# Sandwich network of four blocks on one core: order of work in the block attention and in the three-layer gated network

## The chip, the cores and the metric

One core of one Trainium2 chip. The metric is the device time of one execution of the whole program in microseconds; before the change the median of three runs is 6237.31 us (6226.17 to 6241.25). All data is float32.

## What is computed

The input `x` has 8 batches of 512 rows with 128 features. Four blocks follow one another, each an attention and then a feed-forward part, and each part `f` is applied as `x = x + layernorm(f(layernorm(x)))`. Only the first block is touched by the change. Its two parts, cut to what matters:

```python
def _L0_attn_ref(x, ...):                       # 16 heads of 8 features
    q = rmsnorm(proj(wq_w, wq_b), qn_w)
    k = rmsnorm(proj(wk_w, wk_b), kn_w)
    v = proj(wv_w, wv_b)
    allowed = (i[None, :] <= i[:, None]) & (i[:, None] - i[None, :] < WINDOW)   # WINDOW = 32
    scores = jnp.einsum('bhqd,bhkd->bhqk', q, k) * scale
    attn = jax.nn.softmax(jnp.where(allowed[None, None], scores, -jnp.inf), axis=-1)
    out = jnp.einsum('bhqk,bhkd->bhqd', attn, v)
    return out.transpose(0, 2, 1, 3).reshape(b, l, d) @ wo_w.T + wo_b

def _L0_ffn_ref(x, ...):                        # D_IN = 128, D_HID = 512
    h = jax.nn.silu(_tlin(x, w1_w, w1_s)) * _tlin(x, w2_w, w2_s)
    h = jax.nn.gelu(_tlin(h, h1_w, h1_s), approximate=False)
    h = jax.nn.gelu(_tlin(h, h2_w, h2_s), approximate=False)
    return _tlin(h, w3_w, w3_s)
```

## The kernel before

The whole `x` stays in SBUF. Stages run one after the other, each in a block of its own, and inside a stage each engine has its own list of instructions, written out by hand; an engine waits on semaphores that other engines raise. No planner chooses an order. A stage runs over 8 batches (`B`), a batch being four tiles (`TB`) of 128 rows.

**Block attention** (`stage_attn0`, unrolled over 8 batches and their 32 tiles). The window of 32 keys lets a block of 32 queries see only 64 keys. For a batch, VectorE normalizes `x` (`input_stats`, `input_norm`, with the inverse root on GpSimd), PE transposes it (`turn_input`, L968) into PSUM bank 2, ScalarE copies it (`copy_input`, L1090), PE makes queries and keys (`project`, L975) in banks 2 and 3, VectorE adds the bias and clips (`unscaled`, L1176 and L1180), ScalarE squares (`squares`), VectorE sums (`mean_squares`, L1185 to L1187), ScalarE takes roots (`roots`, L1098), VectorE divides (`scaled`, L1191 and L1192), PE transposes queries and keys back (`turn`, L986), and ScalarE copies the queries once and the keys eight times, each time with other heads masked to zero (`queries` L1102, `keys` L1107). The values are made by `project_v` (L994), again in banks 2 and 3, and copied by ScalarE (`values`, L1114). For a tile, PE makes the scores (`scores`, L1006) in banks 0 and 1, VectorE adds the mask and takes the maximum (`masked`, L1199 and L1202), GpSimd subtracts it (`shifted`, L946), ScalarE takes the exponential (`probs`, L1120), PE transposes (`transposes`, L1015), ScalarE copies (`probs_turned`, L1124), PE multiplies with the values (`values`, L1028) and VectorE divides by the sums (`weighted`, L1207 and L1208). At the end of a batch come `turn_output` (L1040), `copy_output` (L1129), `output` (L1046, bank 2), `result` (L1213) and the output norm (`post`). Two things are waited for across batches: the first scores of a batch wait for all its key copies (`kz_ready`), and `turn` waits until `result` has read bank 2 (`y_read`).

```python
            for n in range(N):
                b, t = n // TB, n % TB
                if t == 2 and b + 1 < B:
                    turn(b + 1)
                if n + 1 < N:
                    scores(n + 1)
                if t == 0:
                    project_v(b)
                if n:
                    values(n - 1)
```

**Gated layer network** (`stage_ffn0`, a loop over the 8 batches on each engine). PE: eight up products in pairs (`w1` and `w2`, L354; chunk `m` of the pair goes to banks `2m % 4` and the next), 16 products of the first hidden layer (L363), the transposes of the next batch's input (L254), 16 of the second, and 16 small down products into bank 4 (L376). ScalarE applies silu to one of a pair (L401), VectorE multiplies it by the other (L443) and so frees that bank; ScalarE applies gelu to the hidden layers (L409). VectorE then takes the result (L451), normalizes it and adds it to `x` before it comes to the next batch's first pair. Silu and gelu need different function tables in ScalarE. `pe.drain()` before a semaphore makes PE wait until its products have left it.

## Time and profile before

| | us |
|---|---|
| median of three runs | 6237.31 |
| lowest and highest run | 6226.17, 6241.25 |
| the profiled execution, its own time | 6221.95 |
| its span | 6220.1 |
| block attention in it, first product to last addition to `x` | 17.04 to 380.27 |
| gated layer network in it, first transpose to last addition | 397.46 to 761.41 |
| PE, VectorE, ScalarE, GpSimd busy in the span | 5232.3, 3558.8, 2288.6, 2504.0 |

The span runs from the first instruction to the last on the slowest core (there is one). A row of a timeline gives the start, the length, the engine, the line of the kernel, what is written from what, how many instructions it merges, and in brackets how long the engine had been idle and who ended that. PE's matmuls in float32 are recorded as two each. DVE is VectorE, ACT ScalarE, POOL GpSimd; PEclk is the clock granted to TensorE, 1.00 being full.

### The profile page before, as it was taken

What the parts mean: (1) busy time and instruction counts of PE and PEld (TensorE: products, weight loads), DVE (VectorE), ACT (ScalarE), POOL (GpSimd) and SP (SyncE); (2) the same over time, 40 slices, a digit from 0 to 9 for tenths busy, and PEclk for the clock granted to TensorE, in tenths of its full rate; (3) what the DMA queues carried; (4) which work ended last, traced back from release to release, by engine and by line L of the source; (5) the groups of instructions that cost most, each with busy time, mean ns of one, the idle gap of its engine ahead of it and who ended that gap; (6) DMA issues with size and microseconds to landing.
All of it is one profiled execution on the core that took longest, in us unless ns stands there. A gap on an engine that the chain in (4) does not pass through costs nothing. (4 is left out here: it accounts for less than half of the span.)

```text
span 6220.1 us, 182529 instructions
## 1 busy us (share of the span) xinstructions
PE 5232.3 (84%) x72132; PEld 3776.6 (61%) x72132; DVE 3558.8 (57%) x9531; ACT 2288.6 (37%) x4072; POOL 2504.0 (40%) x2788
## 2 busy tenths in 40 slices
PE   4568868888848888898888888898679999787998
PEld 2334345555536777777777777777346666576776
DVE  4631268787865565555565565565545545685333
ACT  3532236666623333333333333333222333111333
POOL 1210014444436666666666666666300000573000
PEclk8789989999969999999999999999789999898999
DMA  0000010000000000000000000000010000000000
GB/s 19 2 20 0 2 42 1 0 0 0 0 7 11 11 11 12 12 13 12 11 12 11 11 12 11 11 12 11 7 42 0 0 0 0 4 1 28 0 0 13
DMA packets 29562, 58.05 MB, mean 9 GB/s; under 512 B 7312, under 2 KB 14240, under 8 KB 28704
## 3 DMA queue, kind: packets, MB, share of 16 engines
q1 hardware_dynamic: 28960, 48.86, 2.6%
q8 instruction: 520, 8.52, 0.6%
q14 instruction: 82, 0.67, 0.0%
HBM read 46.75 MB, written 2.10 MB: 8 GB/s over the span
## 5 line engine op out<-in xcount | busy, mean ns | idle before, releaser
L617 PEld LDWEIGHTS psum<-m_wd,m_h 128*128 128x128 f32 x6144 | 805.6, 192 | 485.4 <-issue 484.3
L617 PE MATMUL psum<-m_wd,m_h 128*128 128x128 f32 x6144 | 819.6, 277 | 95.3 <-remote 69.6
L2183 POOL TENSOR_TENSOR e_kd<-e_kd,e_tail 128x512 f32<-128x512 f32 x325 | 368.7, 1135 | 567.7 <-PE psum L2290 554.2
L607 PE MATMUL psum<-xT,m_wa 128*128 (+1 forms) x1032 | 544.3, 610 | 8.4 <-remote 8.4
L607 PE MATMUL psum<-xT,m_wb 128*128 (+1 forms) x1032 | 532.8, 598 | 0.0
L784 DVE SCALAR_TENSOR_TENSOR m_acc<-psum,m_combine,m_acc 128x128 f32<-128x128 f32 x1440 | 403.3, 342 | 224.0 <-PE psum L617 211.0
L544 POOL TENSOR_TENSOR m_h<-m_td,m_tb 128x512 f32<-128x512 f32 x258 | 328.6, 1274 | 468.6 <-DVE m_tb L812 468.6
L2320 PE MATMUL psum<-e_T,e_N 64*64 64x32 f32 x10400 | 407.1, 232 | 67.7 <-remote 66.3
L2320 PEld LDWEIGHTS psum<-e_T,e_N 64*64 64x64 f32 x10400 | 370.6, 148 | 113.2 <-issue 110.0
L2290 PE MATMUL psum<-e_kd,e_k 64*64 64x64 f32 x10400 | 420.1, 237 | 0.3
L143 POOL TENSOR_SCALAR m_post_rstd<-m_post_mv 128x4 f32<-128x4 f32 x27 | 6.2, 228 | 990.7 <-DVE m_post_mv L133 990.7
L2290 PEld LDWEIGHTS psum<-e_kd,e_k 64*64 64x64 f32 x10400 | 372.4, 149 | 6.9 <-issue 1.2
L805 DVE SCALAR_TENSOR_TENSOR m_h<-psum,m_bb,m_ta 128x512 f32<-128x512 f32 x258 | 193.2, 749 | 308.4 <-ACT m_ta L705 305.2
L607 PEld LDWEIGHTS psum<-xT,m_wb 128*128 128x128 f32 x1032 | 199.3, 193 | 253.5 <-issue 253.5
L705 ACT ACTIVATE m_ta<-psum,m_ba 128x512 f32<-128x512 f32 x258 | 177.2, 687 | 458.9 <-PE psum L607 458.8
L2341 PE MATMUL psum<-e_Z,e_TT 64*64 64x32 f32 x8320 | 296.7, 221 | 25.0 <-DVE e_Z L2693 21.1
L2585 ACT ACTIVATE e_T<-psum 128x256 f32<-128x256 f32 x325 | 125.6, 386 | 514.4 <-PE psum L2341 514.4
L2693 DVE COPY e_Z<-psum 64x256 f32<-64x256 f32 x325 | 135.9, 418 | 301.8 <-PE psum L2320 301.5
L2341 PEld LDWEIGHTS psum<-e_Z,e_TT 64*64 64x64 f32 x8320 | 267.5, 135 | 48.7 <-issue 33.5
L699 ACT ACTIVATE m_h<-psum,m_ba 128x512 f32<-128x512 f32 x258 | 177.3, 687 | 288.3 <-PE psum L600 288.3
L2177 POOL TENSOR_TENSOR e_k<-e_k,e_tail 128x256 f32<-128x256 f32 x390 | 281.2, 721 | 0.0
L600 PE MATMUL psum<-m_normed,m_wa 128*128 128x512 f32 x516 | 268.9, 604 | 6.2 <-remote 6.2
(434 smaller groups left out, 11884.4 us busy)
## 6 DMA issues: line engine op xcount, KB each, us to landing
e_w<-in_e_w SPq DMA_DIRECT2D x66, 321.0 KB, 2.9
m_wa<-in_m_wa SPq DMA_DIRECT2D x12, 512.0 KB, 7.5
m_wd<-in_m_wd SPq DMA_DIRECT2D x12, 512.0 KB, 8.7
m_wb<-in_m_wb SPq DMA_DIRECT2D x8, 512.0 KB, 8.8
f_h<-in_f_h SPq DMA_DIRECT2D x2, 1024.0 KB
out<-x SPq DMA_DIRECT2D x1, 2048.0 KB, 8.7
f_w<-in_f_w SPq DMA_DIRECT2D x3, 256.0 KB
g_w<-in_g_w SPq DMA_DIRECT2D x3, 256.0 KB
```

The costliest lines, as they stand in the source:

```text
L544: g.tensor_tensor(h[:, j, :], td[:, j, :], tb[:, j, :], ALU.mult).then_inc(h_ready[j], 1)
L600: pe.matmul(c.ps[u % 4][:], wa[q][:, j, :], nrm[:, e % 2, :], start=True, stop=True).then_inc(a_ready[u % 4], 1)
L607: pe.matmul(c.ps[i][:], w[q][:, j, :], xb, start=True, stop=True).then_inc(a_ready[i], 1)
L617: r = pe.matmul(c.ps[4 + e % 2][:, t * P:(t + 1) * P], h[:, u % DEPTH, t * P:(t + 1) * P], wd[u // UQ][:, u % UQ, :], start=(m == 0 and t ...
L699: a.activation(h[:, j, :], c.ps[u % 4][:], ACT.Relu, bias=ba[:, u:u + 1]).then_inc(h_ready[j], 1)
L784: r = v.scalar_tensor_tensor(to[:, t, :], c.ps[4 + e % 2][:, t * P:(t + 1) * P], comb[:, t, e:e + 1], acc[:, t, :], ALU.mult, ALU.add)
L805: v.scalar_tensor_tensor(h[:, j, :], c.ps[2 * k + 1][:], bb[:, u:u + 1], ta[:, j, :], ALU.add, ALU.mult).then_inc(h_ready[j], 1)
L2177: return g.tensor_tensor(even(k[:], m), even(src[:], m), gate, ALU.mult)
L2183: return g.tensor_tensor(both_odd(dst[:], m), both_odd(src[:], m), gate.unsqueeze(1).broadcast_to((P, 2, nb, m)), ALU.mult)
L2290: r = pe.matmul(c.psum[half(h), G_, chunk(u)], keys[half(h), chunk(u)], both_odd(gated[half(h), :, chunk(u)], 1 << l), start=True, stop=True)
L2320: r = pe.matmul(c.psum[half(1 - h), Z_, u * HC:(u + 1) * HC], N[half(h), l - 1, chunk(u)], even(T[half(h), chunk(u)], 1 << l), start=True, ...
L2341: r = pe.matmul(even(c.psum[half(h), T_, chunk(u)], 1 << l), left[half(h), chunk(u)], Z[half(h), u, :], start=False, stop=False, skip_grou ...
```

## The change

In block attention every engine's list is rewritten. Scores stand two tiles ahead of the transposes instead of one, on PE, VectorE (`masked`) and GpSimd (`shifted`). `turn` of the next batch moves from the third tile to the end of the first; the key copies are spread over the second tile; `project_v` of the next batch moves up into the third tile, before it is needed; `project` moves to the fourth tile, and belongs to the batch after next. The input transposes go to bank 3 in place of bank 2. Output projection, result and output norm come a batch later. In the gated layer network the first pair of up products of the next batch stands in front of the down products, and VectorE and ScalarE do that pair's work at the end of the turn; the scaling of the result, its norm and the addition move into the next batch's turn, behind three of its four pairs. Two semaphores are added there for the banks of the second product of a pair. No operation on data is dropped; one pair of up products, with one silu and one multiplication, is added for a ninth batch that nobody reads.

```diff
             pre.pe(pe, 0)
+            pe.wait_ge(pre.xT_ready, 1)
+            pe.sem_clear(pre.xT_ready)
+            up(0, c.xT[:, 0:L])
             with pe.Fori(0, B) as b:
...
+                for m in range(1, HC):
+                    up(m, c.xT[:, bass.ds(b * L, L)])
                 for n, w in enumerate((h1, h2)):
...
+                pe.wait_ge(pre.xT_ready, 1)
+                pe.sem_clear(pre.xT_ready)
+                up(0, c.xT[:, bass.ds((b + 1) * L, L)])
                 pe.wait_ge(h_ready[2], HC)
...
+            with v.Fori(1, B) as b:
+                ch.reset()
+                for m in range(1, HC):
+                    gated(m)
+                pre.dve_first(v, ch, b + 1)
+                scaled()
                 post.dve_stats(v, ch, lambda t: y[:, t, :])
-                post.dve_add(v, ch, b, lambda t: y[:, t, :])
+                pre.dve_last(v, ch, b + 1)
+                post.dve_add(v, ch, b - 1, lambda t: y[:, t, :])
+                first_gated()
...
             def turn(b):
                 pe.wait_ge(qk_ready, b + 1)
-                if b >= 2:
-                    pe.wait_ge(y_read, b - 1)
+                pe.wait_ge(xT_ready, min(b + 2, B))
+                if b >= 3:
+                    pe.wait_ge(y_read, b - 2)
...
             def project_v(b):
-                pe.wait_ge(xT_ready, min(b + 2, B))
+                pe.wait_ge(kz_ready, b + 1)
...
             for n in range(N):
                 b, t = n // TB, n % TB
+                if t == 3 and b + 2 < B:
+                    project(b + 2)
+                if n + 2 < N:
+                    scores(n + 2)
+                if t == 0 and b >= 2:
+                    output(b - 2)
                 if t == 2 and b + 1 < B:
-                    turn(b + 1)
-                if n + 1 < N:
-                    scores(n + 1)
-                if t == 0:
-                    project_v(b)
+                    project_v(b + 1)
                 if n:
                     values(n - 1)
+                if t == 0 and b + 2 < B:
+                    turn_input(b + 2)
+                transposes(n)
                 if t == 0 and b + 1 < B:
-                    pe.wait_ge(vz_ready, b + 1)
-                    project(b + 1)
-                transposes(n)
...
+                    turn(b + 1)
+                if t == 3 and b:
+                    turn_output(b - 1)
...
             copy_input(0)
+            copy_input(1)
             squares(0)
...
                 if t == 1 and b + 1 < B:
-                    roots(b + 1)
-                if t == 2 and b + 1 < B:
                     queries(b + 1)
-                    keys(b + 1, range(HP // 2))
-                probs_turned(n)
+                    keys(b + 1, range(2))
                 if n + 1 < N:
                     probs(n + 1)
...
+                if t == 1 and b + 1 < B:
+                    keys(b + 1, range(2, 6))
...
+                probs_turned(n)
+                if t == 1 and b + 1 < B:
+                    keys(b + 1, range(6, HP))
```

Three places of the order, word for word. **Block attention on PE, from `turn` (a_qk) to `project` (a_wqk).** Names are what is written and read: a_qk queries and keys, a_kz masked keys, a_wv the value weights, a_xn the normalized input, a_o the attention output. Before:

```order
L986 MATMUL psum<-ident,a_qk 128x128 x8
L1006 MATMUL psum<-a_kz,a_qT 32x512 x8
L1028 MATMUL psum<-a_vz,a_probsT 32x18 x32
L1015 MATMUL psum<-ident,a_probs 128x128 x8
L1006 MATMUL psum<-a_kz,a_qT 32x512 x8
L1028 MATMUL psum<-a_vz,a_probsT 32x18 x32
L1015 MATMUL psum<-ident,a_probs 128x128 x8
L968 MATMUL psum<-ident,a_xn 128x128 x4
L1006 MATMUL psum<-a_kz,a_qT 32x512 x8
L994 MATMUL psum<-a_wv,a_xTp 64x64 x32
L1028 MATMUL psum<-a_vz,a_probsT 32x18 x32
L975 MATMUL psum<-a_wqk,a_xTp 128x256 x4
```

In the changed kernel:

```order
L1036 MATMUL psum<-ident,a_qk 128x128 x8
L1056 MATMUL psum<-a_kz,a_qT 32x512 x8
L1078 MATMUL psum<-a_vz,a_probsT 32x18 x32
L1065 MATMUL psum<-ident,a_probs 128x128 x8
L1056 MATMUL psum<-a_kz,a_qT 32x512 x8
L1044 MATMUL psum<-a_wv,a_xTp 64x64 x32
L1078 MATMUL psum<-a_vz,a_probsT 32x18 x32
L1065 MATMUL psum<-ident,a_probs 128x128 x8
L1024 MATMUL psum<-a_wqk,a_xTp 128x256 x4
```

From `turn` to the next batch's first scores there is now one turn of values and transposes with one scores product before it, as before; but behind those first scores the value products (a_wv) follow at once, where a tile, the input transposes (a_xn) and the second tile's scores stood between. The output transposes and the output projection, which stood ahead of `turn`, stand elsewhere.

**Block attention on ScalarE and VectorE, around the exponentials' table load and around `scaled` (a_qk).** ScalarE before, then changed:

```order
L1120 ACT_TABLE_LOAD
L1120 ACTIVATE a_probs<-a_probs 128x1024
L1102 ACTIVATE a_qT<-psum,a_nw 128x512
L1107 ACTIVATE a_kz<-psum,a_headmask 128x512 x4
L1124 ACTIVATE a_probsT<-psum 128x1024
L1120 ACTIVATE a_probs<-a_probs 128x1024
L1107 ACTIVATE a_kz<-psum,a_headmask 128x512 x4
```

```order
L1153 ACTIVATE a_qT<-psum,a_nw 128x512
L1158 ACTIVATE a_kz<-psum,a_headmask 128x512 x2
L1171 ACT_TABLE_LOAD
L1171 ACTIVATE a_probs<-a_probs 128x1024
L1158 ACTIVATE a_kz<-psum,a_headmask 128x512 x4
L1175 ACTIVATE a_probsT<-psum 128x1024
L1158 ACTIVATE a_kz<-psum,a_headmask 128x512 x2
```

The table load and the exponential now stand among the key copies. VectorE before, then changed:

```order
L1199 TENSOR_TENSOR a_probs<-psum,a_window 128x1024
L1202 TENSOR_REDUCE a_max<-a_probs 128x16
L1207 RECIPROCAL a_rec<-psum 128x16
L1208 TENSOR_TENSOR a_o<-psum,a_rec 128x128
L1191 RECIPROCAL a_rstd<-a_rstd 128x128
L1192 TENSOR_TENSOR a_qk<-a_raw,a_rstd 128x1024
L1213 TENSOR_TENSOR a_y<-psum,a_bo 128x512
```

```order
L1254 TENSOR_TENSOR a_probs<-psum,a_window 128x1024
L1257 TENSOR_REDUCE a_max<-a_probs 128x16
L1246 RECIPROCAL a_rstd<-a_rstd 128x128
L1247 TENSOR_TENSOR a_qk<-a_raw,a_rstd 128x1024
L1262 RECIPROCAL a_rec<-psum 128x16
L1263 TENSOR_TENSOR a_o<-psum,a_rec 128x128
L1268 TENSOR_TENSOR a_y<-psum,a_bo 128x512
```

`weighted` (a_rec, a_o) stood between the maximum and `scaled`, and now stands behind it, with `result` (a_y) last in both.

**Gated layer network on PE, the end of a turn of the loop** (f_w the up and down weights, ISA a drain or a wait with a clear). Before, from the drain behind the second hidden layer:

```order
L366 ISA
L371 ISA
L373 ISA
L376 MATMUL psum<-f_w,f_hid 128x128 x16
L345 REGISTER_ALU
L345 COMPARE_AND_BRANCH
```

Changed:

```order
L379 ISA
L384 ISA
L358 ISA
L359 ISA
L359 MATMUL psum<-xT,f_w 128x512
L358 ISA
L359 MATMUL psum<-xT,f_w 128x512
L387 ISA
L389 ISA
L392 MATMUL psum<-f_w,f_hid 128x128 x16
L366 REGISTER_ALU
L366 COMPARE_AND_BRANCH
```

The pair of up products stands between that drain and the down products.

## Rows read from the trace of the kernel before

**Rows 1.** The stage windows of one batch, attention and gated layer (window, length, busy by engine, PEclk, DMA, GB/s).

```profile
197.00:238.00 41.00, 23.17 (x449) 15.16 (x448) 24.44 (x50) 20.59 (x26) 10.11 (x8) 0.79 0.01 2
534.20:578.60 44.40, 39.65 (x116) 18.93 (x116) 9.12 (x30) 11.41 (x15) 2.53 (x4) 1.00 0.00 0
```

**Rows 2.** PE's timeline over one batch of block attention (start, length, what, xcount, idle before).

```profile
207.19 1.94 PE L986 MATMUL psum<-ident,a_qk 128*128 128x128 f32 x8 [6.50 <-DVEq L1215]
...
219.15 1.96 PE L1006 MATMUL psum<-a_kz,a_qT 64*32 64x512 f32 x16 [5.85 <-ACT a_kz L1107]
...
226.69 1.11 PE L968 MATMUL psum<-ident,a_xn 128*128 128x128 f32 x4 [3.23 <-DVE a_xn L155]
...
229.62 2.08 PE L994 MATMUL psum<-a_wv,a_xTp 128*64 128x64 f32 x64
...
234.02 1.99 PE L975 MATMUL psum<-a_wqk,a_xTp 128*128 128x256 f32 x8 [1.64 <-ACT a_vz L1114]
```

**Rows 3.** PE's timeline at the two ends of block attention.

```profile
68.95 3.61 PE L975 MATMUL psum<-a_wqk,a_xTp 128*128 128x256 f32 x8 [3.36 <-ACT a_vz L1114]
...
95.88 1.96 PE L1006 MATMUL psum<-a_kz,a_qT 64*32 64x512 f32 x16 [5.66 <-ACT a_kz L1107]
...
311.65 3.56 PE L994 MATMUL psum<-a_wv,a_xTp 128*64 128x64 f32 x64
...
343.67 1.96 PE L1006 MATMUL psum<-a_kz,a_qT 64*32 64x512 f32 x16 [6.43 <-ACT a_kz L1107]
...
355.80 1.09 PE L1006 MATMUL psum<-a_kz,a_qT 64*32 64x512 f32 x16
...
359.66 1.09 PE L1006 MATMUL psum<-a_kz,a_qT 64*32 64x512 f32 x16
```

**Rows 4.** ScalarE's timeline in the same batch.

```profile
196.82 1.05 ACT L1120 ACTIVATE a_probs<-a_probs 128x1024 f32<-128x1024 f32 x1
...
199.32 1.28 ACT L1098 ACT_TABLE_LOAD   x1
...
200.84 1.00 ACT L1124 ACTIVATE a_probsT<-psum 128x1024 f32<-128x1024 f32 x1
...
209.17 2.42 ACT L1107 ACTIVATE a_kz<-psum,a_headmask 128x512 f32<-128x512 f32 x4 [0.17 <-PE psum L986]
```

**Rows 5.** VectorE's timeline, the first batch and the same later one.

```profile
50.95 1.22 DVE L1192 TENSOR_TENSOR a_qk<-a_raw,a_rstd 128x1024 f32<-128x1024 f32 x1
...
195.02 1.22 DVE L1176 TENSOR_TENSOR a_raw<-psum,a_bqk 128x1024 f32<-128x1024 f32 x1 [3.04 <-PE psum L975]
196.40 0.69 DVE L1180 TENSOR_SCALAR a_raw<-a_raw 128x1024 f32<-128x1024 f32 x1
198.85 1.22 DVE L1185 TENSOR_REDUCE a_rstd<-a_sq 128x128 f32<-128x1024 f32 x1 [1.75 <-ACT a_sq L1094]
...
200.50 1.22 DVE L1199 TENSOR_TENSOR a_probs<-psum,a_window 128x1024 f32<-128x1024 f32 x1
...
203.00 0.25 DVE L1207 RECIPROCAL a_rec<-psum 128x16 f32<-128x16 f32 x1
...
203.72 0.95 DVE L1191 RECIPROCAL a_rstd<-a_rstd 128x128 f32<-128x128 f32 x1
204.71 1.44 DVE L1192 TENSOR_TENSOR a_qk<-a_raw,a_rstd 128x1024 f32<-128x1024 f32 x1
```

**Rows 6.** GpSimd's timeline, same batch.

```profile
203.17 1.90 POOL L946 TENSOR_TENSOR a_probs<-a_probs,a_max 128x1024 f32<-128x1024 f32 x1 [9.82 <-DVE a_max L1202]
```

**Rows 7.** PE's timeline in one batch of the gated layer.

```profile
540.90 2.84 PE L354 MATMUL psum<-xT,f_w 128*128 x6 [2.10 <-DVEq L445]
...
557.86 0.65 PE L254 MATMUL psum<-ident,f_pre_y 128*128 128x128 f32 x4 [0.38 <-remote]
...
573.84 3.83 PE L376 MATMUL psum<-f_w,f_hid 128*128 128x128 f32 x32 [1.08 <-remote]
578.66 3.69 PE L354 MATMUL psum<-xT,f_w 128*128 x8 [0.98 <-remote]
```

More of the change, by code:

```diff
@@ L317, in stage_ffn0 @@
     free = [s(f"bank{i}_free") for i in range(4)]
+    gate_ready = [s(f"gate{i}_ready") for i in range(2)]
     t_ready = [s(f"silu{i}_ready") for i in range(2)]
@@ L332, in _ @@
             pre.pool(g, ch, 0)
-            with g.Fori(0, B) as b:
+            pre.pool(g, ch, 1)
+            with g.Fori(1, B) as b:
                 ch.reset()
@@ L382, in _ @@
                 pe.sem_clear(free[i])
+            pe.wait_ge(h_ready[0], 1)
+            pe.sem_clear(h_ready[0])
             pe.wait_ge(y_free, 1)
             pe.sem_clear(y_free)
-            pre.drain_pe(pe)
+            pe.wait_ge(pre.t_free, 1)
+            pe.sem_clear(pre.t_free)
         @block.scalar
@@ L413, in _ @@
                         pre.act(a, b + 1)
+                silu(0)
             pre.drain_act(a)
@@ L431, in _, with gated, first_gated, scaled @@
                 v.sem_inc(t_free[i], 1)
-            pre.dve(v, ch, 0)
-            with v.Fori(0, B) as b:
-                ch.reset()
+            def gated(m):
+                i = (2 * m + 1) % 4
+                v.wait_ge(gate_ready[i // 2], 1)
+                v.sem_clear(gate_ready[i // 2])
+                v.wait_ge(t_ready[m % 2], 1)
+                v.sem_clear(t_ready[m % 2])
+                v.scalar_tensor_tensor(hid[0][:, m, :], c.ps[i][:], s2[:, m:m + 1], t_s[:, m % 2, :],
+                                       ALU.mult, ALU.mult).then_inc(h_ready[0], 1)
+                d = v.drain()
+                d.then_inc(free[i], 1)
+                v.sem_inc(t_free[m % 2], 1)
+            def first_gated():
                 v.wait_ge(h_free[0], 1)
                 v.sem_clear(h_free[0])
-                for m in range(HC):
-                    i = (2 * m + 1) % 4
-                    v.wait_ge(ready[i], 1)
-                    v.sem_clear(ready[i])
-                    v.wait_ge(t_ready[m % 2], 1)
-                    v.sem_clear(t_ready[m % 2])
-                    v.scalar_tensor_tensor(hid[0][:, m, :], c.ps[i][:], s2[:, m:m + 1], t_s[:, m % 2, :],
-                                           ALU.mult, ALU.mult).then_inc(h_ready[0], 1)
-                    d = v.drain()
-                    d.then_inc(free[i], 1)
-                    v.sem_inc(t_free[m % 2], 1)
-                pre.dve(v, ch, b + 1)
+                gated(0)
+            def scaled():
                 v.wait_ge(y_ready, 1)
@@ L1153, in _ @@
                 if t == 0 and b + 1 < B:
-                    squares(b + 1)
+                    roots(b + 1)
+                if t == 0 and b + 2 < B:
+                    copy_input(b + 2)
+                if t == 1 and b + 1 < B:
+                    keys(b + 1, range(2, 6))
                 if t == 2 and b + 1 < B:
-                    keys(b + 1, range(HP // 2, HP))
+                    values(b + 1)
                 if t == 3 and b + 2 < B:
-                    copy_input(b + 2)
+                    squares(b + 2)
+                probs_turned(n)
+                if t == 1 and b + 1 < B:
+                    keys(b + 1, range(6, HP))
+                if t == 3 and b:
+                    copy_output(b - 1)
             copy_output(B - 1)
@@ L1237, in _ @@
             masked(0)
+            masked(1)
+            unscaled(1)
+            input_stats(2)
+            input_norm(2)
             for n in range(N):
```

137 lines of the change are left out of this document (77 added, 60 removed).

## Prediction

> **What bounds the kernel now.** I read the stage windows first, then the PE timeline of the two touched stages, then the timelines of the engines that PE waits for. The windows show two different stages [rows 1]. In block attention a batch takes 41.0 us and no engine is full: PE 23.2, VectorE 24.4, ScalarE 20.6, GpSimd 10.1 us, with the granted clock at 0.79. So a chain over several engines bounds it. In the gated layer network PE is busy 39.65 of 44.4 us at clock 1.00: PE bounds it, and only its gaps can be won.
>
> The attention chain is seen by following each long PE gap to its releaser [rows 2]. `turn` starts at 207.19 after 6.50 idle, released by VectorE's `result` (L1215). The next batch's first scores start at 219.15, after 5.85 idle for the last key copy of ScalarE. Then one tile's work and a wait for the normalized input (3.23) follow before the value products at 229.62; `project` follows at 234.02, when ScalarE has copied the values. 41.03 us before the next `turn` is the last one, so I can cut the cycle into legs: turn to first scores 11.96; first scores to value products 10.47; value products to VectorE's bias addition 6.43 (195.02 in the earlier batch [rows 5], so 236.05 here); and from that addition to `turn` 12.17 (195.02 to 207.19). They add up to 41.03.
>
> **Part 1: block attention, per batch.** I lay out the same cycle in the changed order.
>
> *Turn to first scores.* From the start of `turn` to the first key copy stays 1.98 (207.19 to 209.17). ScalarE's queue then holds two key copies (1.21, half of the 2.42 for four), the exp table load (1.28), an exponential (1.05, about 1.0 net, since its successor starts early), four key copies (2.42), a `probs_turned` (1.00), two key copies (1.21) [rows 4]. The exponential's input comes from a tile that GpSimd finished before; the transposes behind `probs_turned` are on PE by then. Sum 1.98 + 8.12 + 0.06 hand-off = 10.16. What goes is the wait between the two halves of the keys; what is new is the table load on this path, which stood beside a GpSimd wait. The load before the roots takes 1.28 and the next but one instruction stands 1.52 behind its start, so nothing follows it [rows 4]. *The Trainium skill, "ScalarE: Activation LUTs", section "What ACT_TABLE_LOAD costs", adds a drain of about 1.38 us to each 1.28 us load; by that, an estimate, each batch would cost 1.4 more and the forecast would be some 8 us later. This trace has no room for it.*
>
> *First scores to VectorE's bias addition.* The scores take 1.96. The value products follow at once: 2.08 usually, 3.56 in the one batch where they ran at the lower of the two clock levels (1.2 GHz instead of 2.4) [rows 2, 3]. The 1.96 of the scores is that level too (1.09 at the other), and in the changed order the value products stand 2.0 us behind the long gap, where they stood 2.9 us behind one (226.69 to 229.62). I take 3.2, nearer the slow row, and keep both ends. From their end to `project` 2.32 (229.62 + 2.08 to 234.02); values and transposes of a tile fit in there. `project` 1.99 plus hand-off 0.04. Sum 1.96 + 3.2 + 2.32 + 2.03 = 9.51. Gone is everything that stood between the first scores and the value products.
>
> *Bias addition to the next turn, all on VectorE* [rows 5]. Addition 1.38 (195.02 to 196.40); clip 0.83 (0.69 and the usual 0.14 to the next); mask, maximum and `weighted` of a tile 3.22 (200.50 to 203.72); sums 1.65 (198.85 to 200.50), their squares being ready while the tile is worked on; a second mask, maximum and weighted 3.22; reciprocal, `scaled` and `result` up to the release of PE 3.47 (203.72 to 207.19). Sum 13.77. That is 1.6 more than the 12.17 of before: two tiles are served now, where one was, but a wait for squares is gone. On top comes contention that the rows show: `scaled` took 1.22 with GpSimd idle (50.95) and 1.44 at 204.71, when GpSimd's subtraction (203.17 to 205.07) still ran; it ended 1.08 behind that. In the changed order `weighted` (0.72) no longer stands between the maximum and `scaled`, so `scaled` starts 0.72 earlier against the same subtraction. If it again ends 1.08 behind, it takes 2.16: +0.72 [rows 5, 6]. At the low end this is 0. Leg: 14.49.
>
> Period: 10.16 + 9.51 + 14.49 = **34.2 us**. The roots' result is due 0.2 us before VectorE wants it, so that wait is hidden, barely; each engine's own work (24.4 at most) stays below. Low end: value products 2.08 and no contention, 32.4. High end: 3.56, and `project` at 3.61 as in the first batch [rows 3]: 36.1.
>
> From batch 1's first scores (95.88) to batch 7's (343.67) there are six periods, 247.8 us [rows 3]. Six at 34.2 are 205.2: **-42.6**. At the start the second batch's input transposes and their copy stand ahead of `turn` and of the squares: +1. At the end the last batch's first scores stand one tile earlier in the list, so one more tile follows them, 3.86 at the tail's pace (355.80 to 359.66), and two output norms are left instead of one, mostly beside it: +4 (0 to 8). The first batches have no `result` and norm yet, which I price at nothing to -2.5. Attention: **-37.6**.
>
> **Part 2: gated layer network** [rows 7]. The first pair of up products moves in front of the down products. (a) The wait of 2.10 in the middle of the up products goes: VectorE came to the first pair only after norm and addition of the last batch. Now it does the pair under the down products (3.83), ScalarE's silu table load included, and result and norm run under the 14 us of hidden products (543.7 to 557.86). Seven times: -14.7. (b) The 1.08 before the down products, a wait for the last gelu, is covered by the pair (2 x 0.87), but the drain ahead of the pair costs what the same drain costs ahead of the transposes, 0.38: saved 0.7 in seven batches, -4.9. (c) In the last batch the pair for nobody takes 1.74 + 0.38 in place of 1.08: +1.0. (d) The 0.98 between down products and up products, drain and loop branch, stays. What is late next: VectorE must finish the next input's norm before the transposes, some 19 us after the turn begins; its work of a whole batch is 9.1 [rows 1]. The silu and gelu loads are as many as before. **-18.6**, with -12 if (b) and part of (a) come back.
>
> Sum: -37.6 - 18.6 = **-56.2**. Against the profiled execution (6221.95) that is 6165.8. That execution lies 15.4 under the median and even under the fastest of the three runs, so I apply the difference to the median: 6237.3 - 56.2 = **6181**.
>
> **The rivals.**
>
> *The clock takes more of it.* Long gaps remain before the first scores and before `turn`, and after each the rows show 1.2 GHz. If most of the chain's PE work stays there, the period is the 36.1 above: six times 1.9 more, 11.4, so 6192. For it: the granted clock of 0.79 and the slow row of 3.56. Against: 2.08 and 1.99 are the usual rows behind gaps of the same size. *The Trainium skill, "TensorE: Matmul & The Clock Gate", part 4, says that transposes do not count as activity for the clock, which speaks for this rival in a stage so rich in them.*
>
> *One half doesn't work.* In the gated network the 2.10 could turn into another wait, since the pair's bank must be freed by ScalarE and VectorE out of the same turn; then only attention gains: 6181 + 18.6 = 6200. Nothing in the rows asks for it: both engines idle there.
>
> *Slower.* One mechanism: engines work in order, and the lead of two tiles puts `masked(n+2)` ahead of `weighted(n-1)` on VectorE, and scores ahead of values on PE. Should each of them wait on the other's newest tile, the lead overlaps nothing, and each tile is a full round: scores 1.96, mask and maximum 2.50, GpSimd 1.90, exponential 1.05, transposes and values at most 2.32 together, copy 1.00, `weighted` 0.72, in all 11.4, four times 45.8, and the key copies (4.84) and the table load (1.28) come in series as ScalarE holds them before the exponential: 51.9 a batch. Six times 10.6 over the 41.3 that the six now take each, +64, +5 at the ends, -18.6: 6287. It decides from a period of some 43.5, where the six periods eat up the gated network's gain. Against it: walked through, only one long wait per batch (for the keys) blocks the scores.
>
> **How the numbers follow.** Forecast, period near 34 and the gated network's gain: 0.72. Clock rival 0.19. Half of it missing 0.06. Slower 0.03. The first three lie over 18.7 us (0.3%, about what a measurement of this kernel can tell from no change) below the median, the third by twice that; with a doubt left for a smaller gain: faster 0.94, same 0.03, slower 0.03. Range: low end, period 32.4 (-10.8), first batches -2.5, tail nothing, and a few us between medians: 6158. High end: the clock rival and half of the gated gain missing, 6202.
>
> **What would show it.** In the changed profile: first scores of the steady batches about 34 us apart; `turn` still released by `result`, and the first scores by the last key copy some 10 us after `turn`; value products directly behind the scores, at 3 us or more if the clock holds low; `scaled` near 2.16; in the gated network a turn of 41.6 us, no wait for VectorE between up products, 0.4 before the moved pair, down products at once behind it. The forecast is wrong if the scores are released by something other than the keys, if the period exceeds 36.1 or falls under 32.4, or if a wait over 1 us stands between hidden products.

## The result, and the profile after

The changed kernel takes 6155.83 us (median of four runs, 6151.69 to 6163.73) against 6231.74 (four runs, one more than were on record ahead of it, 6220.64 to 6241.25): ratio 0.988, 95% interval 0.9859 to 0.9902. The profiled execution took 6151.69 us, its span 6149.9. It is faster, as predicted, and by more than the range allowed: 6155.8 lies 2.2 us below the range's low end of 6158 and 25 us below the forecast of 6181.

A stage is counted below from its first weight transfer to the next stage's first, in SyncE's timeline, the last one to the transfer of the output.

| us | block attention | gated layers | the eight other stages |
|---|---|---|---|
| before | 369.67 | 380.98 | 5449.0 |
| after | 326.62 | 359.03 | 5443.5 |
| difference | -43.1 | -22.0 | -5.5 |

The windows of the changed kernel: attention stage, one batch of it, gated stage, one turn of it, and the delta stage (gated delta attention of a later block, whose code the change does not touch). Columns as in [rows 1]; the busy times are those of PE's products, PE's weight loads, VectorE, ScalarE and GpSimd.

```profile
11.63:338.25 326.62, 178.65 (x3586) 121.32 (x3586) 209.92 (x402) 164.53 (x201) 81.07 (x64) 0.85 0.01 3
220.06:253.91 33.85, 21.39 (x449) 14.85 (x449) 24.23 (x49) 20.31 (x25) 10.14 (x8) 0.85 0.01 2
338.25:697.28 359.03, 319.14 (x936) 154.94 (x936) 74.48 (x253) 93.88 (x123) 22.32 (x34) 0.97 0.02 8
443.44:484.75 41.31, 39.34 (x117) 19.11 (x117) 8.89 (x30) 11.41 (x15) 2.65 (x4) 1.00 0.00 0
1783.68:4308.59 2524.91, 2242.47 (x55182) 1819.03 (x55182) 1487.67 (x3407) 912.49 (x2020) 1603.49 (x1909) 0.94 0.04 12
```

An attention batch takes 33.85 us instead of 41.03, with the same VectorE and ScalarE work (24.2 and 20.3 us busy, 24.4 and 20.6 before). PE is busy 21.4 us in it, 23.2 before, at the higher granted clock; the rest of what went is waiting. PE's timeline over that batch, to be held against [rows 2], and the first scores of the second and the last batch [rows 3]:

```profile
96.00 1.96 PE L1056 MATMUL psum<-a_kz,a_qT 64*32 64x512 f32 x16 [4.16 <-ACT a_kz L1158]
...
220.06 1.94 PE L1036 MATMUL psum<-ident,a_qk 128*128 128x128 f32 x8 [6.66 <-DVEq L1270]
...
230.10 1.38 PE L1056 MATMUL psum<-a_kz,a_qT 64*32 64x512 f32 x16 [4.48 <-ACT a_kz L1158]
231.41 3.33 PE L1044 MATMUL psum<-a_wv,a_xTp 128*64 128x64 f32 x64
...
237.15 1.96 PE L1024 MATMUL psum<-a_wqk,a_xTp 128*128 128x256 f32 x8 [0.72 <-ACT a_vz L1165]
...
298.08 1.96 PE L1056 MATMUL psum<-a_kz,a_qT 64*32 64x512 f32 x16 [4.37 <-ACT a_kz L1158]
```

`turn` to first scores is 10.04 us. The value products now follow the scores at once; the 3.23 us wait of before is gone. From 96.00 to 298.08 there are six periods in 202.08 us, where there were 247.8. In the later profiles of the same two kernels they are 202.1 to 203.7 us in four of the change and 245.6 to 245.8 in three of before, which have no batch like the one of 42.5 us at the end of [rows 3]. The last leg is VectorE's; from its timeline, and GpSimd's, in the same batch:

```profile
239.30 1.22 DVE L1231 TENSOR_TENSOR a_raw<-psum,a_bqk 128x1024 f32<-128x1024 f32 x1
...
249.97 2.16 DVE L1247 TENSOR_TENSOR a_qk<-a_raw,a_rstd 128x1024 f32<-128x1024 f32 x1
...
253.01 0.69 DVE L1268 TENSOR_TENSOR a_y<-psum,a_bo 128x512 f32<-128x512 f32 x1
```

```profile
249.16 1.90 POOL L989 TENSOR_TENSOR a_probs<-a_probs,a_max 128x1024 f32<-128x1024 f32 x1 [3.07 <-DVE a_max L1257]
```

ScalarE's timeline shows the table load that came onto the path between turn and scores:

```profile
223.31 1.28 ACT L1171 ACT_TABLE_LOAD   x1
224.60 1.06 ACT L1171 ACTIVATE a_probs<-a_probs 128x1024 f32<-128x1024 f32 x1
225.57 2.41 ACT L1158 ACTIVATE a_kz<-psum,a_headmask 128x512 f32<-128x512 f32 x4
```

PE's timeline in one gated turn, against [rows 7]:

```profile
443.44 5.41 PE L359 MATMUL psum<-xT,f_w 128*128 x12 [0.88 <-remote]
448.69 13.90 PE L376 MATMUL psum<-f_hid,f_h 128*128 128x512 f32 x32
...
478.37 1.98 PE L359 MATMUL psum<-xT,f_w 128*128 x4 [0.49 <-remote]
480.19 3.73 PE L392 MATMUL psum<-f_w,f_hid 128*128 128x128 f32 x32
484.75 5.41 PE L359 MATMUL psum<-xT,f_w 128*128 x12 [0.83 <-remote]
```

Six products of three pairs run through without the 2.10 us wait, and the down products stand directly behind the moved pair. Down product to down product is 41.35 to 41.39 us in all seven turns; before it was 46.15 once and 44.41 to 44.46 six times.

So both halves did what was forecast, within some microseconds. The open questions were where the surplus of 25 us comes from, whether the lead of two tiles or only the new placement does the work, and which leg limits next.

### The profile page after: what moved, and what is told of

The parts are those of the page before. It is cut to its first block and busy times, and to the rows that moved or that the text cites. A ratio compares the mean times of both kernels' runs of the same rounds, so it can differ in the third digit from the quotient of the medians.

```text
span 6149.9 us, 182566 instructions
## 1 busy us (share of the span) xinstructions
PE 5217.9 (85%) x72136; PEld 3775.9 (61%) x72136; DVE 3560.4 (58%) x9532; ACT 2290.1 (37%) x4074; POOL 2504.0 (41%) x2788
## 5 line engine op out<-in xcount | busy, mean ns | idle before, releaser
L2382 PE MATMUL psum<-e_T,e_N 64*64 64x32 f32 x10400 | 407.7, 232 | 63.9 <-remote 63.2
L2382 PEld LDWEIGHTS psum<-e_T,e_N 64*64 64x64 f32 x10400 | 371.6, 149 | 108.9 <-issue 105.1
L2403 PE MATMUL psum<-e_Z,e_TT 64*64 64x32 f32 x8320 | 298.4, 221 | 30.7 <-DVE e_Z L2755 23.8
```

The lines of the kernel that those rows point to most:

```text
L2382: r = pe.matmul(c.psum[half(1 - h), Z_, u * HC:(u + 1) * HC], N[half(h), l - 1, chunk(u)], even(T[half(h), chunk(u)], 1 << l), start=True, ...
L2403: r = pe.matmul(even(c.psum[half(h), T_, chunk(u)], 1 << l), left[half(h), chunk(u)], Z[half(h), u, :], start=False, stop=False, skip_grou ...
```

## The experiments

**The halves alone, and both kernels again.** `same_again` is the kernel before; `full_again` the changed one; `attn_only` takes every list of the new attention and the old gated network; `gated_only` the reverse. The edit in each half is that part of the diff shown above.

> The kernel before with a blank line added, so the same instructions. Theory A (what the change won beyond its two stages is scatter between executions): ratio 1.000 within 0.2%, and the profile's untouched stages differ from those of the first profile of before by as much as the 5 us that were gained there in the changed kernel, the longest stage (2529 us) by up to 4 us. Theory B (the untouched stages really run faster behind the changed ones): the untouched stages repeat here within 1 us in all.

> Only the attention half of the change. Theory: the attention stage takes 326.6 us (369.7 before, so -43), the gated stage about 381 as before, the total -43 +- 5, ratio 0.993. Its steady batches 33.9 apart. Theory B would find the untouched stages 5 us shorter here too. Rival on the clock: the first two turns of the gated stage (46.2 and 46.1 us before, 44.4 later) become short by what the attention stage leaves behind, then the gated stage takes 377.

> Only the gated half. Theory: the gated stage takes 359 us (381.0 before, so -22), a turn 41.4, the attention stage 369.7 as before, total -22 +- 5, ratio 0.9965. If the slow first two turns are a matter of what the attention stage leaves behind, they stay slow here and the gated stage gains 18 to 19 only; if of the 2.10 wait between up products, they are gone here.

> The whole change again (a blank line added). Theory: attention 326.6, gated 359.0, untouched stages within 5 us of either profile; ratio 0.989 +- 0.002, that is -65 to -75; if the profile's two stages are all that is won, the ratio over many runs comes nearer to -65 (0.9896) than to the -76 first measured (0.988).

Ratios are to the kernel before, run beside them (median 6243.58 us).

| | median us (range) | ratio, 95% | attention | gated | eight others |
|---|---|---|---|---|---|
| same_again | 6245.29 (6232.73 to 6256.71) | 1.0002, 0.9992 to 1.0012 | 368.12 | 381.40 | 5480.4 |
| attn_only | 6184.24 (6182.36 to 6190.8) | 0.9903, 0.9889 to 0.9918 | 328.20 | 381.41 | 5458.8 |
| gated_only | 6208.61 (6200.69 to 6222.62) | 0.9944, 0.9931 to 0.9958 | 370.39 | 359.25 | 5465.1 |
| full_again | 6164.59 (6148.56 to 6173.63) | 0.9872, 0.9856 to 0.9888 | 329.13 | 358.45 | 5454.5 |

The two stages are independent: each half gains in its own stage what the whole gains there. But the medians win more than the stages: 79.0 us against 61.9 (the two stages of `same_again` less those of `full_again`). Each half does the same for itself: `attn_only` wins 59.3 us, 39.9 of them in the attention stage, and `gated_only` 35.0, 22.2 of them in the gated stage. So some 13 to 19 us lie outside the touched stage with either half, and 17 with both: they don't add up like the stages. Neither theory of `same_again` foresaw that kernel's own untouched stages to differ by 31 us between two profiles (5449.0 and 5480.4). The difference lies in stages with the same code; it is taken up at the end of this section.

**Is it the lead of two tiles?** `lead_one` keeps every new placement and gives back the lead, on PE, VectorE and GpSimd.

```diff
-                if n + 2 < N:
-                    scores(n + 2)
+                if n + 1 < N:
+                    scores(n + 1)
```

> The changed kernel with scores, masked and shifted one tile ahead instead of two; every other move stays. Theory: the lead matters, since on ScalarE the key copies and the roots stand behind an exponential whose subtraction is then made in the same turn: turn to last key 13.9 in place of 10.0; value products at once behind it; addition to turn 18.2 in place of 14.7 (the roots come 4.6 behind the mask), period about 39.6, the stage about 38 us longer. Rival (the gain comes from placing turn and the value products alone): period 34 or less.

Its one run took 6251.82 us, with the new gated network in it; the seven of the kernel before beside it took 6225.8 to 6247.09, median 6236.04. The attention stage is what tells: 405.34 us, some 37 more than before's, with a period of 44.1. From PE's, ScalarE's and VectorE's timelines:

```profile
220.78 1.94 PE L1035 MATMUL psum<-ident,a_qk 128*128 128x128 f32 x8 [5.83 <-DVEq L1268]
...
234.80 3.68 PE L1043 MATMUL psum<-a_wv,a_xTp 128*64 128x64 f32 x64 [7.35 <-ACT a_kz L1156]
```

```profile
229.31 1.06 ACT L1169 ACTIVATE a_probs<-a_probs 128x1024 f32<-128x1024 f32 x1 [4.01 <-POOL a_probs L989]
```

```profile
207.83 1.22 DVE L1238 TENSOR_REDUCE a_rstd<-a_sq 128x128 f32<-128x1024 f32 x1 [3.56 <-ACT a_sq L1143]
...
216.80 0.95 DVE L1244 RECIPROCAL a_rstd<-a_rstd 128x128 f32<-128x128 f32 x1 [4.72 <-ACT a_rstd L1147]
...
243.10 1.22 DVE L1229 TENSOR_TENSOR a_raw<-psum,a_bqk 128x1024 f32<-128x1024 f32 x1
```

Without the lead, the exponential that stands between the key copies waits for GpSimd, so the turn-to-keys leg is 14.0 us in place of 10.0. Squares and roots stand behind such waiting exponentials too, so VectorE waits 3.56 and 4.72 us for them. The expected 39.6 held for the first leg only; the last one, from the addition at 243.10 to the next `turn` at 264.89, is 21.8 us where 18.2 was expected, because the wait for the squares was not foreseen. In block attention the placement alone is a loss; the lead makes it pay.

**The gated half taken apart.** `norm_later_only` keeps the result and norm in the next turn and leaves the pair in its old place. A turn's four pairs of up products are in one piece again:

```diff
-                for m in range(1, HC):
+                for m in range(HC):
                     up(m, c.xT[:, bass.ds(b * L, L)])
...
-                pe.wait_ge(pre.xT_ready, 1)
-                pe.sem_clear(pre.xT_ready)
-                up(0, c.xT[:, bass.ds((b + 1) * L, L)])
```

> The changed kernel, whose gated stage has all four up pairs at the head of the turn as before, and only VectorE's result, norm and addition a batch later. Theory (the 2.10 is VectorE's lateness, and the pair in front only covers the last gelu): no wait between up products, the 1.08 before the down products is back, a turn takes 42.2 to 42.4 in place of 41.35, the stage 366. Rival (the pair in front is needed for the 2.10 as well): a turn of 44.4 or a wait of 1 us or more between up products.

Gated stage 363.26 us (366 expected), turns of 42.11 to 42.19. Its one run took 6214.53 us, but 40 us of that stand in a later stage that the edit does not touch (see the last section), so only its gated stage is compared. PE's timeline:

```profile
481.74 3.83 PE L388 MATMUL psum<-f_w,f_hid 128*128 128x128 f32 x32 [1.08 <-remote]
486.54 7.21 PE L359 MATMUL psum<-xT,f_w 128*128 x16 [0.97 <-remote]
```

Sixteen rows without a wait: the 2.10 us were VectorE's lateness, and the pair in front is not needed to remove them. They are 2.3 of the 3.1 us per turn; the pair in front of the down products is the remaining 0.8, by covering the 1.08.

**Which leg limits next?** Four reorderings of the changed kernel: three in one engine's list each, and one that joins two of them. None touches PE's list. `weighted_first` moves `scaled` behind `weighted`, which takes it out of GpSimd's way:

```diff
-                if t == 0 and b + 1 < B:
-                    scaled(b + 1)
                 if n:
                     weighted(n - 1)
+                if t == 0 and b + 1 < B:
+                    scaled(b + 1)
```

> The changed kernel with weighted put back between the maximum and scaled on VectorE. Theory (scaled is held until GpSimd's subtraction ends): scaled takes 1.44 in place of 2.16, weighted's 0.72 stands in front, and the steady period stays 33.85 within 0.1. Rival (scaled is simply slower in the new order): scaled stays at 2.16 and the period grows by 0.7.

```profile
252.31 1.44 DVE L1247 TENSOR_TENSOR a_qk<-a_raw,a_rstd 128x1024 f32<-128x1024 f32 x1
```

`scaled` fell from 2.16 to 1.44 and the stage stayed (329.31 us, period 34.1, where five profiles of the change have 326.6 to 329.5 and periods of 33.5 to 34.6 from the third batch on; 6154.11 us in one run): what the operation saves, it starts later. The 0.72 of contention is real time, and moving `weighted` alone does not win it back.

`exp_first` puts the next tile's exponential at the head of ScalarE's work for a tile, so it and its table load leave the way to the keys:

```diff
             for n in range(N):
+                if n + 1 < N:
+                    probs(n + 1)
...
-                if n + 1 < N:
-                    probs(n + 1)
```

> The changed kernel with the second tile's exponential, and with it the exp table load, in front of the queries and the first two key copies on ScalarE, where it waits 4.8 us for turn. Theory (these 1.28 + 1.0 stand on the path from turn to the first scores): turn to first scores 10.0 falls to 7.7, the period 33.85 to 31.6, the stage by 14 to 16 us, ratio to before 0.986. Rival (the path there is set by the transposes or by GpSimd): the first scores do not come earlier, period 33.5 or more.

```profile
209.56 1.94 PE L1036 MATMUL psum<-ident,a_qk 128*128 128x128 f32 x8 [6.65 <-DVEq L1270]
...
218.26 1.34 PE L1056 MATMUL psum<-a_kz,a_qT 64*32 64x512 f32 x16 [2.27 <-ACT a_kz L1158]
```

6150.34 us (6139.68 to 6156.94), ratio 0.9864 (0.9843 to 0.9885); attention 310.02, period 31.8. The stage is 17 to 20 us shorter than the change's, but the ratio can't be told from the change's own (0.9866 to 0.988 in three comparisons). The leg is 8.7 us instead of the 7.7 expected, because the last two key copies stand behind a `probs_turned` that now waits 0.92 for its transposes.

`result_first` moves `result` ahead of `scaled` and puts `weighted` last on VectorE; `both_first` adds the edit of `exp_first` to it. `change_beside` is the changed kernel on the same chip.

> The changed kernel, but in block attention VectorE takes the result of the batch before the last in front of the scaling of the next batch's queries and keys, and the weighted sum behind the scaling. In the changed kernel the turn of a batch starts when that result has been read, which stands behind the scaling (2.16 us, of which 0.72 to 0.94 are lost while GpSimd's subtraction runs) and the weighted sum. Theory (the loop over turn, scores and bias addition sets the period, and its last stretch ends in VectorE's list): with the result off the way to the turn, only the scaling is left; the wait of the turn then ends at the scaling, and 14.61 from the addition to the turn becomes 12.9 to 13.8; the period goes from 33.85 to 32.2 to 33.2 us, the attention stage from about 328 to 317 to 324 us. Rival (the period is set by VectorE's own amount of work, 24.2 busy of 33.85, in any order): the weighted sum then comes later, the value chain behind it too, and the period stays within 0.3 us of 33.85.

> The version meant to beat both kernels: the exponential of the next tile in front of ScalarE's other work of a tile (which gave a period of 31.8 us in place of 33.85), and on VectorE the result in front of the scaling, the weighted sum behind it. Theory: the two lie on different legs of the same loop, so their gains add: period 30.1 to 31.2 us, first part of the program (block attention) 298 to 306 us, whole kernel 6130 to 6145 us in the profile and a ratio to before of 0.982 to 0.986. Rival (another bound takes over at once, VectorE with 24.2 us of work and its waits, or GpSimd): no more than with the exponential alone, period 31.8, attention 310, ratio 0.9864.

> The changed kernel itself beside the two above, on the same chip. Expected as in the first comparison: attention stage 326 to 330 us, gated stage 358 to 360 us, ratio to before 0.986 to 0.989. If what the medians win beyond the two stages (about 14 us) belongs to the change, the untouched stages of this profile lie near the changed kernel's 5443 to 5455 us; if it is scatter of executions, they may as well lie at 5465 to 5480 as in the kernel before's second profile.

PE's timeline, `result_first`, then `both_first`:

```profile
215.97 1.97 PE L1036 MATMUL psum<-ident,a_qk 128*128 128x128 f32 x8 [5.24 <-DVEq L1249]
...
248.62 1.97 PE L1036 MATMUL psum<-ident,a_qk 128*128 128x128 f32 x8 [4.99 <-DVEq L1249]
```

```profile
209.88 1.97 PE L1036 MATMUL psum<-ident,a_qk 128*128 128x128 f32 x8 [5.24 <-DVEq L1249]
...
240.53 1.97 PE L1036 MATMUL psum<-ident,a_qk 128*128 128x128 f32 x8 [4.99 <-DVEq L1249]
```

`turn` is now released by L1249, the end of `scaled`, in place of `result` (L1270). Periods: 32.65 and 30.65 us in the rows shown. `result_first` took 6155.36 us in its one run. Stages: 320.01 and 307.80, the latter a little above the 298 to 306 expected: in `exp_first` the third turn came 28.2 us after the second, here 30.7, so an early batch gives back 2.5 of what the later ones win. The two gains add in the steady batches, so VectorE's amount of work (24.2 us in the change's batch) is not yet the bound. `both_first` took 6148.47 us (6145.56 to 6154.08), ratio 0.9842 (0.9816 to 0.9868), with 6165.34 (6151.03 to 6175.03), 0.9866 (0.984 to 0.9891), for the change beside it. It is 17 us better than the change at the medians, with the lowest ratio found; its interval overlaps those of `exp_first` and of the change, and the profiled run, 6150.03, missed the 6130 to 6145 expected. That the attention stage is shorter is shown (307.80 against 329.52); how much of it the whole kernel keeps is known only roughly.

**Where the surplus is.** Four more profiles, two of each kernel:

> The kernel before once more, for its profile. Theory A (what the medians win beyond the two touched stages is scatter of executions): the eight untouched stages last 5443 to 5481 us in any profile of either kernel, and the means of the two kernels agree within 5 us. Rival (the change also shortens the untouched stages, by some 12 to 15 us, through what state it leaves behind): the kernel before stands at 5465 to 5480, the changed kernel at 5443 to 5458, and 5449.0 in the first profile of before was its low outlier. Both: attention stage 368 to 370, gated stage 381 us.

> The changed kernel once more, for its profile. Both theories: attention stage 326 to 330 us, gated stage 358 to 360 us. Theory A (scatter): untouched stages anywhere in 5443 to 5481 us. Rival (the change shortens them): 5443 to 5458 us again.

> As the other look at the kernel before: scatter puts its untouched stages anywhere in 5443 to 5481 us, the rival at 5465 to 5480.

> As the other look at the changed kernel: scatter puts its untouched stages anywhere in 5443 to 5481 us, the rival at 5443 to 5458.

Their single runs took 6254.94 and 6265.84 us (before), 6156.77 and 6172.63 (change). With the earlier profiles of the same code:

| us | the eight others | of these, delta stage | PE idle for "issue" in it |
|---|---|---|---|
| before, four profiles | 5449.0, 5480.4, 5483.9, 5493.2 | 2529.0, 2546.0, 2549.9, 2559.9 | 24.6 to 30.4 |
| change, five profiles | 5443.5, 5454.5, 5457.5, 5447.3, 5464.4 | 2524.9, 2523.0, 2526.6, 2518.5, 2525.3 | 11.0 to 15.6 |

The scatter theory asked for means within 5 us of each other. They differ by 22.5 us in the delta stage and by 23 over all eight stages, though nothing in them was touched, so it falls, even if the delta stages come close at one end: the change's longest is 2526.6, before's shortest 2529.0. The two halves have 2530.4 and 2530.2 there, with 18.7 and 17.9 us of issue idle. What differs most clearly is "issue": idle time of PE for which the profile shows no wait, 12.6 us less at the mean. PE's busy time in the stage is less too, by 15 us at the mean (2254.0 and 2238.9), at a granted clock of 0.93 or 0.94. So the last three kernels move PE's later code by instructions without work:

```diff
+            for _ in range(8):
+                pe.drain()
             pe.wait_ge(y_free, 1)
             pe.sem_clear(y_free)
```

once, behind the loop of the gated stage, with 8 or 100 drains in the kernel before and 100 in the changed one.

> The kernel before with eight more drains in PE's list, once, at the end of the gated layer stage. They cost under 1 us there and move all of PE's later code by eight instructions. Rival (the delta stage's 2529 to 2560 us before and 2517 to 2530 after are a matter of where PE's code lies): the idle that the trace puts down to issue in the delta stage leaves 24.6 to 30.4 us for the changed kernels' 10 to 19, and the stage comes to 2517 to 2530 us. Theory (it is another thing that the two stages leave behind, not PE's code position): issue idle stays at 24 to 31 us and the stage above 2540 us.

> As the one with eight drains, with a hundred: a drain without work costs at most some tens of ns, so at most a few us at the end of the gated stage. By code position the delta stage's issue idle comes out at another value than 24.6 to 30.4 us; by the other theory it stays.

> The changed kernel with a hundred drains at the same place. By code position its issue idle in the delta stage leaves the 11 to 16 us of the changed kernel's profiles, in either direction, and the stage's length with it; by the other theory both stay (2518 to 2527 us).

| | run us | delta stage | issue idle |
|---|---|---|---|
| before_pad8 | 6227.32 | 2522.0 | 11.9 |
| before_pad100 | 6248.49 | 2539.2 | 21.5 |
| change_pad100 | 6192.66 | 2545.4 | 22.3 |

The groups of PE's instructions by line over the delta stage show it. Last column: idle time before them and its parts. First `before_look2`, then `before_pad8`, then `change_pad100`:

```profile
L2434 PE MATMUL psum<-e_headmask,e_sq 128*128 128x2 f32 x1056 | 132.3, 255 | 8.3 <-issue 6.0 <-ACT e_kn L2567 2.3
...
L2380 PE MATMUL psum<-e_bv,e_TTH 64*64 64x64 f32 x1040 | 80.0, 227 | 11.3 <-issue 11.3
```

```profile
L2436 PE MATMUL psum<-e_headmask,e_sq 128*128 128x2 f32 x1056 | 130.1, 254 | 2.3 <-ACT e_kn L2569 2.3
...
L2380 PE MATMUL psum<-e_bv,e_TX 64*64 64x64 f32 x1040 | 78.2, 222 | 4.1 <-issue 4.1
...
L2382 PE MATMUL psum<-e_bv,e_TTH 64*64 64x64 f32 x1040 | 77.1, 223 | 0.0
```

```profile
L2355 PE MATMUL psum<-e_kdn,e_kn 64*64 64x64 f32 x2080 | 78.0, 224 | 24.7 <-remote 16.5 <-issue 8.2
```

The edit adds two lines, so L2380 of the first fence is L2382 in the second. With eight instructions ahead the 11.3 us of issue idle are gone from that product, and 4.1 stand before its neighbour; the 6.0 before the `e_sq` product are gone too. In the padded changed kernel 8.2 us stand before another product altogether, which had none in the other two. Without padding, these places repeat: 11.3 to 12.1 us before that `e_TTH` product in all four profiles of before, 0.7 or less in all nine profiles with the changed PE list (five of the change, four of the reorderings, which have 9.7 to 14.7 us of issue idle in all). So what stands ahead of the loop in PE's list sets how long, and where, the same loop idles without a wait shown.

How far the time follows is less sure. There is one profile of each padded kernel. Two lie outside what their kernel showed otherwise in the length of the delta stage: 2522.0 against 2529 to 2560, and 2545.4 against 2518 to 2527; `before_pad100` lies inside before's spread in length, though below it in issue idle. The whole runs say less: the unpadded kernel before took 6229.63 us beside them, on the same chip, 2.3 us more than `before_pad8`, and no profile was taken of it there. So that `before_pad8` is short because of its padding, and not because the kernel before ran short on that chip, is not shown by its time. `change_pad100` lies 18 us above the slowest of all runs of the change. The time also moves by more than the issue idle: the delta stages of `before_look2` and `before_pad8` differ by 27.8 us, of which 13.6 is issue, and PE's busy time is longer too (the windows give the delta stage 2258 us at granted clock 0.93, against 2240 at 0.94). The 2529.0 of before's first profile had 24.6 us of issue idle but the clock of 0.94, and `lead_one` the reverse: 10.3 us of issue idle, the clock of 0.93, and 2530.4 us. So both take part. That the change's own gain there comes from the shift of PE's code is the reading that fits best (a hundred drains take it back); it is shown for the issue idle, about half of the gain, and not for the busy time and the clock. How code position makes PE wait was not tried.

## Why the prediction missed

**Attention, chain and legs: right.** Turn to first scores 10.04 (10.16 forecast); scores to bias addition 9.20 (9.51), with value products of 3.33 where 3.2 was chosen between 2.08 and 3.56; addition to turn 14.61 (14.49), `scaled` at 2.16 exactly. The period is 33.85 for 34.2; `turn` released by `result`, first scores by the last key copy, as said. The six periods brought -45.7 for -42.6, the tail +2.75 for +4, the start +0.9 for +1. The first interval, from 60.23 to 96.00, was 35.8 us for 36.8 before, and had been priced at nothing. Stage: -43.1 for -37.6. Part of that surplus is this pair of profiles: before's held the batch of 42.5 us, and over all profiles (four and five) the stage's means differ by 40.3.

**Gated layers: right in mechanism, small by 3.4 us.** The turn is 41.35, 41.6 forecast. 2.0 of the miss is 0.28 in each of seven turns. Another 1.7 us is a patch I had left out. In one turn the 2.10 wait was followed by six rows in 4.45 us, where other turns take 2.84, which made that turn 46.15 (one turn, not two as the expectation of `attn_only` has it). PE's timeline of the kernel before, that turn and the next:

```profile
450.38 4.45 PE L354 MATMUL psum<-xT,f_w 128*128 x6 [2.10 <-DVEq L445]
...
496.49 2.84 PE L354 MATMUL psum<-xT,f_w 128*128 x6 [2.10 <-DVEq L445]
```

With the wait gone the patch is gone, in the change and in `gated_only`; `attn_only` keeps it (46.15), and `same_again` has it two turns later (46.10, its first at 44.45). The last term, the pair for nobody and the ends, was 1.3 for 1.0.

**The rivals.** The clock rival (36.1) did not come: the granted clock rose from 0.79 to 0.85 in the batches shown and from 0.79 to 0.82 over the six periods. More of PE's work than before runs at the 2.4 GHz level (why was not tried); what stands right behind the gaps (`turn`, value products, `project` at 1.96) still shows 1.2 GHz. *The rule of the Trainium skill, "TensorE: Matmul & The Clock Gate", part 4, that transposes are no activity for the clock, would have made it the likelier; no run here isolates the transposes, and the period it pointed to was not seen.* Neither half failed. The slower case named the right danger in the wrong kernel: in order and without overlap, 51.9 forecast, it is `lead_one` that comes to 44.1 us, over the deciding 43.5, and its attention stage is longer than before's. With the lead, its waits are absent. *The drain of 1.38 us that the Trainium skill, "ScalarE: Activation LUTs", section "What ACT_TABLE_LOAD costs", adds to a load isn't there either: the exponential starts at 224.60, 0.01 after the load's end.*

**The step that failed** is the last one: "That execution lies 15.4 under the median [...] so I apply the difference to the median." The profiled time was forecast at 6165.8 and came out at 6151.7; of these 14.1 us, 5.5 are attention, 3.4 the gated layers, and 5.5 the stages I had taken as fixed (0.2 the other way stands outside the stages). The other 11 us are that sentence. It took the gap between profile and median as belonging to any kernel, while after the change it is 4.1. Before's profile had the shortest delta stage of its four (2529 against 2546 to 2560), so the usual run of before held a loss in untouched stages which that profile's length hardly showed, and which the change's runs don't have. Over all profiles the means differ by 40.3 us in attention, 22.7 in the gated layers and 23 in the eight others, forecast at 37.6, 18.6 and nothing: the failed term is the nothing. About half of it is issue idle that goes with where PE's code lies; the cause of the rest stays open. No edit of the diff was priced for what it does to code behind it, and the range took "a few us between medians" for it where the delta stage alone shows 22.5 at the means. Why the change's first runs are even among its fast ones (6155.8, later 6164.6 and 6165.3) I put down to scatter: the stage of mixed experts ahead of the delta stage took 867 to 884 us in the nine profiles of the two kernels, with both ends of that among the changed kernel's or within 1.2 us of them.

## What to carry to other kernels

Where no engine is full, cut one period into legs between releases and lay the new order out leg by leg with measured durations; the three legs here came within 0.31 us. An order that puts long chains between an engine's short jobs pays only if what it waits for is a full tile ahead: with a lead of one the attention stage took 37 us more than before, with the same placement and a lead of two 40 less. And before carrying a profile's difference to a median, take several profiles and compare the stages that the edit leaves alone; of a gain of 1.2% here some 0.3% lay in stages that nobody touched.

## What the runs showed of the hardware

- PE's idle time for "issue" in a loop of 2520 to 2560 us depends on where its code lies: 24.6 to 30.4 us in four profiles of one kernel, 11.9 with eight empty instructions ahead of it, 21.5 with a hundred (one profile each). The idle moves to other instructions. The stage's length, which differs by up to 41 us between profiles of these kernels (2518.5 to 2559.9), follows it only in part: 2529.0 us with 24.6 of issue idle, 2530.4 with 10.3.
- `scaled` on VectorE ends 1.07 or 1.08 us behind the end of GpSimd's subtraction in the profiles where they overlap: it is recorded as 2.16 (the change: start 249.97, subtraction until 251.06), 1.44 (`weighted_first`: 252.31, until 252.67), 1.33 (`result_first`) and, with GpSimd idle, 1.22 [rows 5]. The wait stands in the operation's own duration, not in its idle time.
- Behind a wait of 2.10 us among matmuls the next six rows took 1.6 us longer in one turn, and no longer in the six others with the same wait. Which turn it is changes between executions of the same instructions.
- In `norm_later_only` an untouched later stage (the second of mixed experts) took 779.0 us where all others took 738.7 to 739.0. Of these 40 us, 24.6 are seven waits of PE for VectorE (L841), which the same stage of before doesn't have, and 15 are PE's busy time, at a granted clock of 0.96 where before has 0.98. Why they came stays open.
